# Rotated queries and keys copied from their staging tile straight to the stacks in SBUF, queries first in each chunk

## The reference

```
q = (x @ Wq)                         # 16 heads x 16 values; k and v come from a latent of 64
c_kv = x @ Wkv_down;  k = c_kv @ Wk_up;  v = c_kv @ Wv_up
q, k: the last 12 of 16 values of each head are rotated by cos/sin of the position
weights = softmax(causal(q k^T / 4));  out = weights v
x = layernorm(x + out)
x = layernorm(x + experts(x))        # top 2 of 16 experts, and 2 shared ones
```

## Time and profile before

| | |
|---|---|
| median of 3 runs | 842.92 us (840.75 to 847.7) |
| profiled execution, its own time | 841.11 us |
| its span in the profile | 839.4 us |
| attention, by PE's last score product | to 564 us |
| PE busy | 729.1 us, 87% of the span |
| DVE, ACT, POOL busy | 561.3, 403.3, 243.8 us |
| DMA moved | 76.99 MB, mean 92 GB/s |

### The profile page before, as it was taken

How to read it: one execution, slowest core, us unless ns; L and a number is a source line. 1 busy time by engine, 2 the same in 40 slices (tenths; PEclk the granted TensorE clock), 3 DMA queues, 4 the chain that set the end, 5 groups by cost and what they waited for, 6 DMA issues and landing times. The chain is left out here.

```text
span 839.4 us, 14305 instructions
## 1 busy us (share of the span) xinstructions
PE 729.1 (87%) x4309; PEld 491.7 (59%) x4310; DVE 561.3 (67%) x1374; ACT 403.3 (48%) x891; POOL 243.8 (29%) x327
## 2 busy tenths in 40 slices
PE   4579899999999999999999999992879999999930
PEld 4467675764755665566465656441469966667610
DVE  6745777878788877776878788103574455666645
ACT  3124463655665756676656667781423322222203
POOL 6316182341261043107100000111027413333323
PEclk9659898999999999999999999995799999999975
DMA  4754326140052006002500000004997223323244
GB/s 130 177 150 117 87 49 180 38 120 22 2 140 88 1 2 145 8 1 55 148 2 1 1 2 1 2 1 161 319 288 269 94 67 93 101 89 100 88 158 173
DMA packets 43596, 76.99 MB, mean 92 GB/s; under 512 B 5984, under 2 KB 23136, under 8 KB 42672
## 3 DMA queue, kind: packets, MB, share of 16 engines
q1 hardware_dynamic: 35919, 57.72, 25.3%
q0 software_dynamic: 5184, 14.72, 5.1%
q10 hardware_dynamic: 2432, 3.80, 1.2%
HBM read 42.40 MB, written 33.45 MB: 90 GB/s over the span
## 5 line engine op out<-in xcount | busy, mean ns | idle before, releaser
L560 ACT ACTIVATE probs<-scores 128x512 f32<-128x512 f32 (+3 forms) x609 | 288.3, 545 | 183.3 <-PE scores L689 167.5
L782 DVE TENSOR_REDUCE mx<-turn_ps 128x1 f32<-128x512 f32 (+3 forms) x576 | 304.8, 591 | 74.2 <-PE turn_ps L652 74.1
L652 PE MATMUL turn_ps<-k_stack,q_stack 96*128 96x512 f32 (+3 forms) x832 | 250.6, 365 | 14.0 <-issue 4.2
L689 PE MATMUL scores<-q_stack,k_stack 98*128 98x512 f32 (+3 forms) x609 | 232.9, 396 | 10.7 <-ACT probs L560 6.0
L652 PEld LDWEIGHTS turn_ps<-k_stack,q_stack 96*128 96x128 f32 x832 | 152.2, 202 | 90.4 <-issue 34.7
L689 PEld LDWEIGHTS scores<-q_stack,k_stack 98*128 98x128 f32 x609 | 117.8, 195 | 43.4 <-ACT probs L560 24.1
L709 PE MATMUL pv_ps<-probs,v_ones 128*17 128x512 f32 (+3 forms) x1280 | 135.4, 539 | 1.2 <-POOL probs L467 0.8
L467 POOL TENSOR_SCALAR_AFFINE_SELECT probs<-probs 128x512 f32<-128x512 f32 x64 | 40.6, 635 | 325.1 <-ACT probs L560 324.9
L1154 POOL DMA_INDIRECT token_y<-ys,dest x47 | 45.5, 968 | 99.2 <-DVE ys L1519 56.8
L709 PEld LDWEIGHTS pv_ps<-probs,v_ones 128*17 128x17 f32 x1280 | 29.2, 97 | 67.1 <-issue 33.4
L1276 PE MATMUL gu_ps<-w_up_sb,xg_t 128*128 x188 | 67.2, 480 | 0.4 <-ACT xg_t L1213 0.3
(11 more groups left out here) (159 smaller groups left out, 767.5 us busy)
## 6 DMA issues: line engine op xcount, KB each, us to landing
kq_split<-kq_stage SPq DMA_DIRECT2D x96, 128.0 KB, 2.4
k_stack<-kq_split SPq DMA_DIRECT2D x8, 768.0 KB, 6.2
q_stack<-kq_split SPq DMA_DIRECT2D x32, 192.0 KB, 4.8
xg<-slot_x SPq DMA_DIRECT2D x47, 130.0 KB
slot_x<-blank SPq DMA_DIRECT2D x11, 520.0 KB, 7.8
w_up_sb<-w_up SPq DMA_DIRECT2D x4, 1408.0 KB
w_dn_sb<-w_dn SPq DMA_DIRECT2D x4, 704.0 KB
x_raw<-xT SPq DMA_DIRECT2D x4, 512.0 KB, 5.7
```

What stands on the lines that cost most here:

```text
L560: nc.scalar.activation(probs[:, s % PROB_BUFS, h, off:CH], score_bank(n)[:, off:CH], ACT.Exp)\
L652: ins = nc.tensor.matmul(dst[:, at:at + keys], q_stack[0:STACK, u % 4, h, tile * P:(tile + 1) * P], k_stack[0:STACK, pair, kb * CH + k0:kb ...
L689: nc.tensor.matmul(score_bank(n)[:, off:CH], k_stack[:, 2 * g + h // 2, b * P:(b + 1) * P], q_stack[:, u % 4, h, off:CH], start=True, stop ...
L782: last = nc.vector.tensor_reduce(mx[:, u % 2, h * TPC + tile, column:column + 1], bank_of(bank)[:, at:at + keys], AX.X, ALU.max)
```

## The change

The DRAM tensor `kq_split` is gone. Each piece goes from `kq_stage` to its stack by six DMAs inside SBUF, of 128 KB as before: 64 rows of the staging tile are read and 16 rows of a stack are written, four runs of 2 KB in each. A piece of queries now waits as a whole, until the scores of both units whose slots it takes are done. In each chunk queries come ahead of keys in all engines' lists, `w_q` is loaded ahead of `w_k` and `w_v`, and of chunk 0's first two pieces ACT issues half of the copies. The units' `max_unit` waits for six DMAs a piece.

```diff
-            def load_q(u):
-                c, g = divmod(u, UNITS_PER_CHUNK)
-                m, j0 = g // 2, GH * (g % 2)
...
-                if u >= 4:
-                    sp.wait_ge(pe_scores, GH * first_step[u - 3])
...
-            def store_piece(c, n):
...
+        def stack_piece(eng, c, n, halves=(0, 1)):
+            piece, m, is_q = 4 * c + n, n // 2, n % 2 == 0
+            eng.wait_ge(kq_ready, 2 * (piece + 1))
+            if is_q and c:
+                eng.wait_ge(pe_scores, GH * first_step[(c - 1) * UNITS_PER_CHUNK + 2 * m + 2])
+            elif is_q:
+                eng.wait_ge(zeros_high if m else zeros_low, 1)
+            for two in halves:
+                src = slice(two * (P // 2), (two + 1) * (P // 2))
+                for copy, part in enumerate((0, 1, 0) if is_q else (0, 0, 1)):
+                    rows = slice(two * SPLIT + copy * DH, two * SPLIT + (copy + 1) * DH)
+                    dst = q_stack[rows, 2 * m:2 * m + 2, two::2, :] if is_q else \
+                        k_stack[rows, GH * m:GH * (m + 1), c * CH:(c + 1) * CH]
+                    eng.dma_start(dst.bitcast(F32), kq_stage[src, piece % 2, part].bitcast(F32))\
+                       .then_inc(q_stacked if is_q else k_stacked, 16)
...
-                        store_piece(job[1], job[2] // 2)
-                        if job[1] == 0 and job[2] % 4 == 3:
-                            load_q(job[2] // 4 * 2)
-                            load_q(job[2] // 4 * 2 + 1)
+                        stack_piece(sp, job[1], job[2] // 2, (0,) if job[1] == 0 and job[2] < 4 else (0, 1))
...
-                    pool.wait_ge(kq_stored[piece % 2], 16 * 6 * (piece // 2))
+                    pool.wait_ge(k_stacked if piece % 2 else q_stacked, 16 * 6 * (piece // 2))
...
-            act.dma_start(w_raw[:, OFF_K:OFF_V], t["w_k"]).then_inc(w_loaded[1], 16)
-            act.dma_start(w_raw[:, OFF_V:2048], t["w_v"]).then_inc(w_loaded[1], 16)
             act.dma_start(w_raw[:, OFF_Q:OFF_D].rearrange("p (k n) -> p k n", k=KT),
-                         t["w_q"].rearrange("(k p) n -> p k n", p=P)).then_inc(w_loaded[2], 16)
+                         t["w_q"].rearrange("(k p) n -> p k n", p=P)).then_inc(w_loaded[1], 16)
+            act.dma_start(w_raw[:, OFF_K:OFF_V], t["w_k"]).then_inc(w_loaded[2], 16)
+            act.dma_start(w_raw[:, OFF_V:2048], t["w_v"]).then_inc(w_loaded[2], 16)
...
+                    if job == ("rope", 0, 3):
+                        stack_piece(act, 0, 0, (1,))
+                    if job == ("value", 0, 0):
+                        stack_piece(act, 0, 1, (1,))
...
-                    m, is_q = piece // 2, piece % 2
+                    m, is_q = piece // 2, piece % 2 == 0
...
-                pe.wait_ge(k_stacked, 16 * (2 * c + g // 2 + 1))
-                pe.wait_ge(q_stacked, 16 * 2 * (u + 1))
+                pe.wait_ge(k_stacked, 16 * 6 * (2 * c + g // 2 + 1))
+                pe.wait_ge(q_stacked, 16 * 6 * (2 * c + g // 2 + 1))
```

More of the change, by code:

```diff
@@ L136, in build_attention @@
         aux_at[-1].insert(len(projection_jobs(0)), ("latent", 1, 0))
-    q_load_at = {}
-    for u in range(4, UNITS):
-        c, g = divmod(u, UNITS_PER_CHUNK)
-        projected = next(s for s in aux_at if ("rope", c, 4 * (g // 2) + 3) in aux_at[s])
-        q_load_at[u] = max(first_step[u - 3], projected + 1)
-        assert first_bank_at[u] > q_load_at[u], u
     split_x_at = {}
@@ L184, in build_attention @@
     last_shared = [[j for j in turns[:first_alone] if j in of][-1] for of in (by_act, by_dve)]
-    kq_dram = nc.dram_tensor("kq_split", (NCH, 4, 2, 3, DH * GH, CH), F32, kind="Internal").ap()
     with ExitStack() as ctx:
@@ L248, in build_attention @@
         tok_loaded = sem("tok_loaded")
-        kq_stored = [sem("k_stored"), sem("q_stored")]
         k_stacked = sem("k_stacked")
@@ L385, in _ @@
                             load_tables(job[1] + 1)
-                for u in range(4, UNITS):
-                    if q_load_at[u] == s:
-                        load_q(u)
             sp.wait_ge(x1_stored, 16 * NCH)
@@ L495, in _ @@
             nc.scalar.activation(x_split[:, 0], x_raw[:], ACT.Copy).then_inc(hi_ready, 1)
-            for n, (lo, hi, full) in enumerate(((OFF_D, OFF_K, 16), (OFF_K, 2048, 32), (OFF_Q, OFF_D, 16))):
+            for n, (lo, hi, full) in enumerate(((OFF_D, OFF_K, 16), (OFF_Q, OFF_D, 16), (OFF_K, 2048, 32))):
                 act.wait_ge(w_loaded[n], full)
@@ L525, in read_aux @@
                     nc.scalar.activation(rope_raw[:, k % RAW_BUFS], bank_of(job), ACT.Copy,
-                                         scale=SCALE if (n // 2) % 2 else 1.0).then_inc(act_read, 1)
+                                         scale=1.0 if (n // 2) % 2 else SCALE).then_inc(act_read, 1)
                 else:
@@ L594, in projection @@
                     piece, half = n // 2, n % 2
-                    m, is_q = piece // 2, piece % 2
+                    m, is_q = piece // 2, piece % 2 == 0
                     cols = slice(256 * half, 256 * half + 256)
-                    if n == 0:
+                    if n == 2:
                         wait_read(pe, ("latent", c, 0))
@@ L761, in _ @@
             nc.vector.tensor_tensor(x_split[:, 1], x_raw[:], x_split[:, 0].bitcast(F32), ALU.subtract).then_inc(x_ready, 1)
-            for n, (lo, hi) in enumerate(((OFF_D, OFF_K), (OFF_K, 2048), (OFF_Q, OFF_D))):
+            for n, (lo, hi) in enumerate(((OFF_D, OFF_K), (OFF_Q, OFF_D), (OFF_K, 2048))):
                 dve.wait_ge(hi_ready, n + 2)
@@ L802, in read_aux @@
                     if job[1]:
-                        dve.wait_ge(pe_aux, aux_no[("rope", job[1] - 1, 5)])
+                        dve.wait_ge(pe_aux, aux_no[("rope", job[1] - 1, 7)])
                         dve.wait_ge(dve_read, by_dve[("latent", job[1] - 1, 0)])
```

## The result

The changed kernel took **854.39 us** (median of five runs, 852.05 to 859.1) against 840.75 (837.61 to 847.7) for the kernel before on the same chip: **1.0146 times** as long, 95% interval 1.0112 to 1.018. A second series on another chip gave the same ratio, 1.0146 (1.0102 to 1.019). The forecast was 854.

What follows compares the result with a forecast made beforehand. The prediction took PE, busy 87% of the span, to bound the kernel. Its terms, 841.1 + 10.1 + 5.0 + 3.0 - 4.0, gave 855 us, shaded to 854, with a range of 838 to 864.

Steps and rivals of the forecast that it cites:

- The price of a copy: Each 128 KB copy into 16 rows: 1.21 us, geometric mean of 0.66 and 2.26; twelve behind one wait, 16.2 us.
- Stall at unit 4: Unit 4's first bank waits for twelve copies, landing at 100.4 against 90.32: +10.1 us; the half clock behind only moves.
- Stall at unit 8: Unit 8's first bank waits for copies landing at 195.0 against 190.02: +5.0 us, plus 3.0 for half clock.
- The opening: Before and around the first scores: first score 2.0 us sooner, full clock sooner; together -4 us, between 0 and -9.
- rival 3: Opening: copies at issue pace and clock back at the twelve-matmul run near 48; 835 or 834 us; chance 0.10.
- Elsewhere no stall: Units 6, 10, 12 and 14: copies land before their first banks, so no stall; no us charged.
- rival 2: Copies go at issue pace, 0.64 us: unit 4 +3.3 us, unit 8 no stall; 840 us; chance 0.23.
- Rival 4: Copies at the slow end, 2.26 us each: stalls at units 4, 6, 8 and 12; about 900 us; chance 0.06.

Runs made afterwards that it cites:

- kernel 2: Changed kernel, but each copy writes every sixth row of the stacks' 96 instead of sixteen neighbouring rows; 879.32 us, ratio 1.0047 to the kernel before.
- 9: Changed kernel, but each copy writes every second row of a block of 32; one execution, 847.57 us, where the kernel before has 843.3.
- kernel 11: Number 6 with queries first in chunk 1 too, SP issuing that chunk's keys ahead of the wait; 868.53 us, ratio 0.9897 to the kernel before.
- 4: Changed kernel, but keys ahead of queries on all engines in chunks 1 to 3; 875.52 us, ratio 0.999 to the kernel before.
- number 6: Changed kernel with every-sixth-row copies, keys first in chunks 1 to 3 and SP issuing all copies; 831.74 us, ratio 0.9878 to the kernel before.
- 7: Number 6, but ACT issues its half of chunk 0's first pieces; 835.96 us, ratio 0.9931 to the kernel before.
- number 12: Number 6 run again unchanged, on another chip; 867.24 us, ratio 0.992 to the kernel before.
- 1: Changed kernel, but in chunks 1 to 3 SP issues the keys' copies ahead of the wait for scores; 885.78 us, ratio 1.0121 to the kernel before.
- 3: Changed kernel with every-sixth-row copies and SP issuing keys' copies ahead of the wait in chunks 1 to 3; 874.07 us, ratio 0.9971 to the kernel before.
- kernel 5: Changed kernel, but SP issues all copies and ACT none; 850.09 us, ratio 1.0091 to the kernel before.
- 8: Changed kernel run again word for word, on another chip; 853.74 us, ratio 1.0146 to the kernel before.
- 10: Number 6, but queries first in all chunks and keys' copies issued ahead of the wait; 835.76 us, ratio 0.9927 to the kernel before.

## Why the prediction was right, and where it was not

The time was right to 1 us, and attention nearly: +14.1 by the terms (10.1 + 8.0 - 4.0), +11.0 found in the second trace (8.7 + 3.4 - 7.2, with 5.2 for the masks and 0.9 elsewhere; +16.4 in the first). The two stalls were foreseen where they came and as they came. That the sum is so close is partly luck: one term was too large, one gain too small, and one term was missing.

- **The price of a copy** was 1.21 us with bounds 0.66 and 2.26; measured 1.02 to 1.04 apart, with 3.3 us from the first issue to the first landing where the sum has 2.9 (1.21 + 1.7; the earlier trace rows have a median of 2.4 where I read 2.3, which is 0.1 of it). Last score to last landing: 14.84 for 16.2. That the geometric mean of two far rows came so near is luck, since neither row is like a copy into 16 rows. Kernels 2 and 9 show the reason that I gave, that fewer rows are slower, only half right: sixteen rows are slow if they are neighbours.
- **Stall at unit 4**: +10.1 forecast, +8.7 found; 11.68 us idle for 13. Right, as was the claim that the half clock only moves; after the bank it runs 4.1 us (to 96.3) in the changed kernel and ran 5.9 (to 96.2) before.
- **Stall at unit 8**: 3.69 us idle for 5.0, and half clock from 198.7 to 202.1. I charged 3.0 for the clock by analogy with unit 4, where it was half for 5.9 us after the stall; here it was for 3.4. Together +3.4 (+4.2 in the first trace) for +8.0. This is the mis-sized term of the stalls.
- **The opening**: -4 forecast within 0 to -9 (its parts, -2.0, -1.4, +0.9 and -2, make -4.5), -7.2 at step 8. First score at 51.83 (51.4 forecast), job 4 at 28.06 (27.1), split of x done at 34.7 (33.6), first bank 37.49 (36.6 to 37): each of them 0.4 to 1.1 us late, of which 0.8 is there when ACT's second group of copies goes out, at 24.78 and not 24.0. What was off is the clock. I had it full "near 57", and it was at 51.9, behind the twelve query matmuls at 47.18 and not behind the run after step 0. In the five traces with keys first in chunk 1 it came back at 59.9 to 65.5. But kernels 2 and 11 have the same run of twelve at 47.21 and 43.83 and got it at 59.6 and 56.6, so this run may bring it and does not always. My rival 3 had the early clock, with the range's -9, and a price of a copy that did not come.
- **"Elsewhere no stall"** is the step that failed. The banks of units 6, 10 and 12 wait for nothing, as forecast. At unit 12 that was a near thing and not for my reason: I let the copies start with the last score (312.1 in the kernel before), but the queries' piece itself is split by POOL only at 329.44 in the changed kernel, after the last score at 326.86, and the keys' piece later still, so the last copy lands 1.4 us ahead of the bank. And I asked only who waits for copies. Queries first also shifts the exponentials against POOL's list, where masks stand between whole rotations, 4.2 us for a mask and what follows it:

```profile
114.55 0.64 POOL L430 TENSOR_SCALAR_AFFINE_SELECT probs<-probs 128x512 f32<-128x512 f32 x1 [0.81 <-ACT probs L527]
...
118.76 0.64 POOL L430 TENSOR_SCALAR_AFFINE_SELECT probs<-probs 128x512 f32<-128x512 f32 x1
...
123.00 0.64 POOL L430 TENSOR_SCALAR_AFFINE_SELECT probs<-probs 128x512 f32<-128x512 f32 x1
```

  The kernel before has the same block, and no gap in it:

```profile
106.92 0.64 POOL L467 TENSOR_SCALAR_AFFINE_SELECT probs<-probs 128x512 f32<-128x512 f32 x1 [2.89 <-ACT probs L560]
...
111.13 0.64 POOL L467 TENSOR_SCALAR_AFFINE_SELECT probs<-probs 128x512 f32<-128x512 f32 x1
```

  In the changed kernel POOL waits 0.81 us at 114.55 for exponentials, and all that follows is late by it; PE then waits 1.79 us at 123.78 for the mask of 123.00. The exponentials are late because the queries' two jobs of twelve matmuls now stand in steps 11 and 12, where the keys' jobs of four stood:

```profile
104.73 1.65 PE L577 MATMUL turn_ps<-x_split,w_split 128*128 128x256 f32 x12
...
108.60 1.58 PE L577 MATMUL turn_ps<-x_split,w_split 128*128 128x256 f32 x12
```

  Steps 11 and 12 take 9.3 us and not 7.7, and steps 13 and 14, which have the keys' jobs now, 6.7 and not 8.5. So PE is back in time at step 16, while POOL, whose block starts late and has no slack, is not: the mask of 123.00 comes 17.7 us after unit 3's first (105.28), where it came 16.2 after it before (119.57 and 103.39). Four such waits are new, 5.6 us in all, three of them in the stretches called masks above, which cost +5.2 (+8.1 in the first trace). The traces of kernels 4, 6, 7 and 12, which take the order back, have none of the four; those of 1, 2, 3, 5, 8, 9 and 10, which keep it, have all four, each within 0.05 us of these; 11 has the first two.
- **Rivals**: 2 (copies at the pace of issue) gave 840 us, and kernel 2, which has them so, took 1.0047 times the time before, about 845. Most of the difference is the masks (6.1 us in the three stretches), which rival 2 lacks as the forecast did. Rival 4 is refuted by the price.

What stays open: why the clock comes back at different times in like kernels. With queries first it was full at 45.6 to 51.9 in seven traces but at 59.6 in kernel 2 and at 56.6 in kernel 11.

## What to carry to other kernels

Ask of a transfer not only its bytes and its row count but whether its rows are neighbours: the same 128 KB into sixteen rows took 1.02 us side by side and no more than 0.64, the pace of issue, with every second row. When stores move behind a wait that only loads stood behind, price the whole chain from the release to the last landing, and look at every place where the queue may then stand behind something else (unit 12 here). And when an order changes, read the queue of every engine beside the changed work: here an engine that is 28% busy made PE wait, because its work lies in one block without a gap. A release that you name should be checked as well: at unit 12 it was POOL's split of the piece and not the scores.

## What the runs showed of the hardware

Which rows are written decides the rate of a copy inside SBUF from 64 rows: 132 GB/s into sixteen neighbouring rows with a DMA share of 1.09, 205 and 206 into rows six or two apart with shares of 0.65 and 0.62. The two latter are the pace of issue; what such copies could reach was not measured.

The same idle time does not cost the same clock. Kernels 6 and 12 are the same program, and among unit 5's last banks, in step 20, PE waits 2.1 us for DVE in both:

```profile
127.31 0.55 PE L618 MATMUL turn_ps<-k_stack,q_stack 96*128 96x128 f32 x2 [2.08 <-DVE mx L742]
```

```profile
129.31 0.90 PE L618 MATMUL turn_ps<-k_stack,q_stack 96*128 96x128 f32 x2 [2.07 <-DVE mx L742]
```

In number 6 the clock is half from 128.2 to 131.6, in number 12 from 129.1 to 142.8. The stretch from step 19 to 34 takes 56.3 us in one and 62.1 in the other, and 62.2 in kernel 9. A difference of 6 us between two traces says nothing alone, then; I have leaned on the stretches where all traces of a kind agree.

Issues of DMAs on ACT hold back its computing: six of them, with the wait for POOL's split that three stood behind, put off job 4's rotation by 2.7 us in the opening (kernel 5), and taking them away was worth 4.1 us of attention (kernels 6 and 7).
